# Turning the second attention's queries on VectorE and by way of memory, with scores one step later

## The reference, cut to what matters

```python
def _L1_xattn_ref(text, features, Wq_w, Wq_b, Wk_w, Wk_b, fn_w, qn_w, kn_w):
    features_n = rmsnorm(features, fn_w)
    Q = rmsnorm(jnp.einsum('btd,fd->btf', text, Wq_w) + Wq_b, qn_w)
    K = rmsnorm(jnp.einsum('bsd,fd->bsf', features_n, Wk_w) + Wk_b, kn_w)
    scores = jnp.einsum('btf,bsf->bts', Q, K) * (1.0 / jnp.sqrt(512))
    attn = softmax(scores)
    return jnp.einsum('bts,bsf->btf', attn, features_n)

x = x + tanh(g_xattn[1]) * _L1_xattn_ref(_layernorm(x), ctx, ...)
x = x + tanh(g_ffn[1]) * _L1_ffn_ref(_layernorm(x), ...)
```

## Time and profile before

| | us |
|---|---|
| median of 3 runs (956.25 to 958.32) | 958.04 |
| the profiled execution, its own time | 957.18 |
| its span on the core | 955.4 |
| query loop on TensorE, first matmul to the last `attended` in it | 861.6 to 900.9 |
| end of the last matmul | 952.1 |

### The profile page before, as it was taken

The page is one execution under the profiler, slowest core; times in us unless marked ns, Lnnn a source line. Parts: engine busy times, 40 slices in busy tenths (PEclk is TensorE's granted clock), DMA queues, the critical chain, the costliest instruction groups (busy, mean ns, idle before and its releaser), DMA issues.

```text
span 955.4 us, 15358 instructions
## 1 busy us (share of the span) xinstructions
PE 938.4 (98%) x4818; PEld 790.3 (83%) x4818; DVE 594.3 (62%) x1020; ACT 403.7 (42%) x1088; POOL 497.2 (52%) x463
## 2 busy tenths in 40 slices
PE   9999899999999999999999999999999999999998
PEld 7888688788878887888888888888888888888885
DVE  4788845385538553854476546664576967756754
ACT  5765424352434233433334334433442336657730
POOL 3857753454446453746374636563546335698630
PEclk9999999999999999999999999999999999999999
DMA  7146676875687667776777676866786565232002
GB/s 284 45 147 227 233 254 247 264 267 200 240 270 276 226 241 252 269 259 241 242 259 270 251 235 231 292 241 233 251 280 251 221 227 190 121 105 94 1 1 89
DMA packets 71412, 203.64 MB, mean 213 GB/s; under 512 B 10192, under 2 KB 24784, under 8 KB 70352
## 3 DMA queue, kind: packets, MB, share of 16 engines
q1 hardware_dynamic: 70368, 201.87, 59.3%
q10 hardware_dynamic: 1008, 1.32, 0.4%
HBM read 176.95 MB, written 26.21 MB: 213 GB/s over the span
## 4 chain that ended last, share of the span: by engine, by line
PE 72%; DMA 9%; DVE 9%; POOL 3%; issue 3%; ACT 2%; SPq 2%; DVEq 0%; POOLq 0%; ACTq 0%
PE bank L1965 22%; PE bank L2042 16%; PE bank L1981 9%; DMA keyed<-passing 7%; PE bank L2146 7%; PE bank L2014 6%; PE bank L1998 5%; PE bank L1941 3%; DVE turned_blocks L1435 2%; SPq L452 1%; DVE kt L1475 1%; PE bank L2170 1%; DVE turned_blocks L1439 1%; PE bank L2026 1%; PE bank L2291 1%
## 5 line engine op out<-in xcount | busy, mean ns | idle before, releaser
L2042 PE MATMUL bank<-wvo,ao 128*128 128x512 f32 x768 | 179.8, 391 | 0.6 <-issue 0.6
L1981 PE MATMUL bank<-wvo,ct 128*128 128x512 f32 x768 | 177.8, 390 | 0.0
L1981 PEld LDWEIGHTS bank<-wvo,ct 128*128 128x128 f32 x768 | 143.5, 188 | 29.4
L2042 PEld LDWEIGHTS bank<-wvo,ao 128*128 128x128 f32 x768 | 142.9, 188 | 29.8 <-issue 0.7
L629 POOL TENSOR_TENSOR wvo<-stage,wvo 128x512 fp32r<-128x512 f32 x64 | 85.0, 1350 | 149.6 <-ACT wvo L932 149.6
L1965 PE MATMUL bank<-ring,wkq 128*128 128x512 f32 x648 | 157.3, 390 | 0.0
L1965 PEld LDWEIGHTS bank<-ring,wkq 128*128 128x128 f32 x648 | 121.2, 188 | 25.1
L1453 DVE SCALAR_TENSOR_TENSOR acc<-bank,gated_rows,acc 128x512 f32<-128x512 f32 x128 | 93.2, 742 | 39.3 <-PE bank L2042 38.3
L978 ACT ACTIVATE bank<-bank,nmax 128x128 f32<-128x128 f32 x256 | 88.3, 351 | 55.6 <-DVE nmax L1415 55.6
L1444 DVE TENSOR_TENSOR ao<-bank,ao 128x512 fp32r<-128x512 f32 x64 | 43.9, 691 | 107.1 <-ACT ao L984 107.1
L1475 DVE TENSOR_TENSOR qt<-bank,qt 128x512 f32<-128x512 f32 x98 | 66.4, 690 | 57.1 <-PE bank L1965 55.7
(11 more groups left out here) (186 smaller groups left out, 1508.9 us busy)
## 6 DMA issues: line engine op xcount, KB each, us to landing
ring<-combined SPq DMA_DIRECT2D x216, 512.0 KB, 6.4
stage<-in_w SPq DMA_DIRECT2D x63, 512.0 KB, 4.2
passing<-turned_blocks SPq DMA_DIRECT2D x24, 512.0 KB, 2.9
keyed<-passing SPq DMA_DIRECT2D x96, 128.0 KB, 3.2
combined<-work SPq DMA_DIRECT2D x16, 512.0 KB, 3.6
xraw<-in_x SPq DMA_DIRECT2D x2, 1024.0 KB, 11.8
bias<-in_bias SPq DMA_DIRECT2D x8, 256.0 KB, 4.6
cs<-in_ctx SPq DMA_DIRECT2D x1, 2048.0 KB, 7.7
```

What stands on the lines that cost most here:

```text
L1981: mm = pe.matmul(bank[un_of[m][u] % RING][:, :], ct[:, i, c, b * P:(b + 1) * P], wvo[:, j, c, :], start=(c == 0 and i + j == 0), stop=(c = ...
L2042: mm = pe.matmul(bank[to][:, :], ao[:, h, p, b * P:(b + 1) * P], wvo[:, j, 2 * pair + h, :], start=(h == 0 and p + j == 0), stop=(h == 1 a ...
```

## The change

The four TensorE transposes and the ScalarE copy of each query tile are taken out. `query(u)` now writes `qbr` without regrouping (the regrouping is in the way the next step reads). VectorE turns the tile in 32 by 32 blocks into a new buffer `qtb` with two places (`query_turned(u)`). SyncE stores each tile to `passing_queries` (512 pieces of 512 B), waits until it has landed, and issues four reads of 32 partitions into `qtr`, now with four places. These instructions stand in SyncE's list behind the loop over the keys and ahead of the stores of the result. `query_turned(u)` waits, from u = 2 on, until the store of tile u - 2 has landed. In `qtr` the four chunks of features are interleaved, so that `scored` now loads its 128 by 128 operand with a step of 16 B between neighbours, where they were next to each other.

Everything from the scores on comes one step later: `scored` lags three steps, `probs_turned` four, `attended` five, and the steps of the other engines likewise. After the loop, one more step of each is done, and `base(0)` and `base(1)` come earlier in relation to the scores of tile 7 and the attention of tile 6.

```diff
+                sp.wait_ge(S["k_mm"], B)
+                for u in range(B):
+                    sp.wait_ge(S["q_T"], u + 1)
+                    sp.dma_start(passing_queries[u, :, :, :, :].rearrange("i k j c -> (i k) j c"),
+                                 qtb[:, u % 2, :, :, :].rearrange("p j t c -> p j (t c)")).then_inc(s_qpassed, 16)
+                    if u >= 4:
+                        sp.wait_ge(S["s_mm"], u - 3)
+                    sp.wait_ge(s_qpassed, B + 16 * u + 16)
+                    for j in range(4):
+                        sp.dma_start(qtr[32 * j:32 * j + 32, u % 4, :, :].rearrange("k (i t) c -> k i (t c)", i=4),
+                                     passing_queries[u, :, :, j, :].rearrange("i k c -> k i c")).then_inc(S["q_out"], 16)
...
-                def query_out(u):
-
-                    act.wait_ge(S["q_T"], u + 1)
-                    if u >= 2:
-                        act.wait_ge(S["s_mm"], u - 1)
-                    act.activation(qtr[:, u % 2, :, :], bank[6][:, :].rearrange("p (c t) -> p c t", c=KC),
-                                   ACT.Copy).then_inc(S["q_out"], 1)
...
+                    dve.tensor_tensor(qbr[:, u % 2, :], bank[2 + u % 2][:, :], rows[:, R_BQ, :], ALU.add).then_inc(S["q_b"], 1)
+
+                def query_turned(u):
+
+                    dve.wait_ge(S["q_b"], u + 1)
+                    if u >= 2:
+
+                        dve.wait_ge(s_qpassed, B + 16 * (u - 1))
+                    dve.transpose(qtb[:, u % 2, :, :, :].rearrange("p j t c -> p j c t"),
+                                  qbr[:, u % 2, :].rearrange("p (j c k) -> p j c k", j=4, c=KC)).then_inc(S["q_T"], 1)
...
-                def queries_turned(u):
-
-                    pe.wait_ge(S["q_b"], u + 1)
-                    if u:
-                        pe.wait_ge(S["q_out"], u)
-                    else:
-                        pe.wait_ge(s_dev, x1_done(6))
-                    turned(6, qbr[:, u % 2, :], "q_T")
-
                 def scored(u):
 
-                    pe.wait_ge(S["q_out"], u + 1)
+                    pe.wait_ge(S["q_out"], 64 * u + 64)
...
-                        mm = pe.matmul(bank[0][:, 0:P], qtr[:, u % 2, c, :], kt1[:, u // 2, :, c, u % 2 * 32:u % 2 * 32 + 32],
+                        mm = pe.matmul(bank[0][:, 0:P], qtr[:, u % 4, :, c], kt1[:, u // 2, :, c, u % 2 * 32:u % 2 * 32 + 32],
```

More of the change, by code:

```diff
@@ L183, in build @@
     passing_keys = nc.dram_tensor("passing_keys", (B // 2, 4, 32, 4, KC * 2 * 32), fp32, kind="Internal").ap()
+    passing_queries = nc.dram_tensor("passing_queries", (B, 4, 32, 4, 32 * KC), fp32, kind="Internal").ap()
     expanded = nc.dram_tensor("expanded", (P, KC, D), fp32, kind="Internal").ap()
@@ L217, in build @@
     wra = nc.alloc_sbuf_tensor_at("wra", [P, 2, KC, RAW], fp32r, offset=xr_at)
+    qtr = nc.alloc_sbuf_tensor_at("qtr", [P, 4, P, KC], fp32, offset=xr_at + 8192)
     wt_f = place("wt_f", [P, 2, KC, D], fp32r)
@@ L232, in build @@
     qbr = place("qbr", [P, 2, D], fp32)
-    qtr = place("qtr", [P, 2, KC, P], fp32)
+    qtb = place("qtb", [P, 2, 4, 32, KC], fp32)
     wexp = place("wexp", [P, HB, NEXP, ROUT], fp32)
@@ L327, in build @@
         s_kpassed, s_kback = s_mneg, s_k0
+        s_qpassed = s_css
         half = lambda s: slice(s * 512, s * 512 + 512)
@@ L876, in _ @@
                         split_lo("ra", u - 1)
-                for u in range(4, B):
+                for u in range(3, B):
                     add_row(u - 1, R_BASE, "xn2", "rsb")
@@ L1321, in _ @@
                 probs_out(6)
+                normed(4, 2)
                 normed(5, 2)
@@ L1601, in query @@
                         dve.wait_ge(S["q_ss"], u - 1)
-                    dve.tensor_tensor(qbr[:, u % 2, :].rearrange("p (c j k) -> p j c k", c=KC, j=4),
-                                      bank[2 + u % 2][:, :].rearrange("p (j c k) -> p j c k", j=4, c=KC),
-                                      rows[:, R_BQ, :].rearrange("p (j c k) -> p j c k", j=4, c=KC), ALU.add).then_inc(S["q_b"], 1)
+                    dve.tensor_tensor(qbr[:, u % 2, :], bank[2 + u % 2][:, :], rows[:, R_BQ, :], ALU.add).then_inc(S["q_b"], 1)
[5 more added lines that the diff above has]
+                                  qbr[:, u % 2, :].rearrange("p (j c k) -> p j c k", j=4, c=KC)).then_inc(S["q_T"], 1)
                 def scores_max(u):
@@ L1821, in _ @@
                     query(u)
+                    query_turned(u)
                     if u < 6:
@@ L1827, in _ @@
                         key_turned(7)
-                    if u >= 2:
-                        scores_max(u - 2)
-                    if u >= 4:
-                        x3(u - 4)
-                    if u >= 2:
-                        scores_sum(u - 2)
-                    if u >= 4:
-                        stats1(u - 4, 2)
+                    if u >= 3:
+                        scores_max(u - 3)
+                    if u >= 5:
+                        x3(u - 5)
+                    if u >= 3:
+                        scores_sum(u - 3)
+                    if u >= 5:
+                        stats1(u - 5, 2)
+                scores_max(5)
+                x3(3)
+                scores_sum(5)
+                stats1(3, 2)
                 lo(1, 2)
@@ L2256, in adapters @@
                     elif u == 2:
-                        pe.wait_ge(S["q_out"], B)
+                        pe.wait_ge(s_dev, x1_done(6))
                     elif u == 3:
@@ L2311, in _ @@
                         T(0, 2)
-                    if u:
-                        queries_turned(u - 1)
-                    if u >= 2:
-                        scored(u - 2)
                     if u >= 3:
-                        probs_turned(u - 3)
+                        scored(u - 3)
                     if u >= 4:
-                        attended(u - 4)
+                        probs_turned(u - 4)
+                    if u >= 5:
+                        attended(u - 5)
+                scored(5)
+                probs_turned(4)
+                attended(3)
                 T(1, 2)
                 adapters(0)
-                queries_turned(7)
                 scored(6)
@@ L2327, in _ @@
                 adapters(1)
+                base(0)
                 scored(7)
@@ L2330, in _ @@
                 attended(5)
-                base(0)
                 T(3, 2)
+                base(1)
                 probs_turned(7)
@@ L2335, in _ @@
                 attended(6)
-                base(1)
                 adapters(3)
```

25 lines of the change are left out of this document (12 added, 13 removed).

## The result

The changed kernel takes 970.9 us (median of 4 runs, 969.9 to 973.6) where the kernel before took 958.1 on the same chip: a ratio of 1.0137, 95% interval 1.0112 to 1.0161, 12.8 us slower. The profiled execution took 969.9 us, its span is 968.1. The forecast was 964.3 with a range of 960 to 970: the sign held, but the loss is twice the 6.3 us forecast, and the time is 0.9 us outside the range.

A forecast was written before the change was run, and what follows sets the result against it. TensorE's list was taken as the bound, paced by SyncE's query transfers: new waits of nearly 10 us less 3.5 for transposes end it 6.3 later, 958.0 + 6.3 = 964.3 us, range 960.0 to 970.0.

The forecast's parts named there:

- What bounds the kernel: TensorE, busy 98% of the span: in the query loop a matmul removed is time won, a new wait time lost.
- SyncE's transfers pace TensorE at tiles 5 and 6: End of the query loop: serial query transfers make TensorE wait again; tile 6 decides, last matmul at 958.4 us.
- The sum after `scored(0)`: TensorE's work from the start of the first scores to the end of the last matmul: 72.5 us.
- The transposes, -3.5: TensorE's path in the query loop: four transposes removed per tile save 0.44 us, eight tiles 3.5 us.
- The weight load: Rival, scores on TensorE: loads with the 16 B step make a pair take 0.22 us, 968 in all; chance 0.18.
- VectorE's strided row: Profile row cited against slow strided access: a VectorE operation writing every eighth word, 64 of them, takes 0.22 us.
- The rival's second sum: Scores on TensorE, load and matmul without any overlap: 0.30 us a pair, giving 968 and 15 us.
- The first wait, 5.9: Before the first scores: TensorE is ready at 876.6 us, the first query there at 882.5, a wait of 5.9 us.
- The rate of the queries, 4.5: SyncE's queue: each query takes 2.3 us to store and 2.2 to issue its reads, a period of 4.5 us.
- The store's 2.6 us: A query's store to memory by the Trainium skill's rule, 2.6 us, beside the 2.3 that the forecast took.
- The clock: TensorE's clock was at the full level in all 40 slices, so the forecast counted no term for it.
- Its wait for the stores: VectorE's turning of a query waits for the store of tile u - 2; claimed to cost nothing while reads are slow.

The follow-up runs named there:

- quarter kernel: The kernel before with one of the four TensorE transposes of each query tile, three left out: 953.9 us, ratio 0.9969.
- the join is soon: The kernel after with chunks kept apart, ScalarE's joining copy ahead of its exponentials, the weighting of the last keys later: 966.0 us.
- the best kernel: The kernel after with chunks apart, joined by ScalarE ahead of exponentials, first queries' transfers ahead of the last keys, some VectorE work later: 957.1 us.

## Why the prediction was right in its sign and short in its size

**What bounds the kernel: right.** TensorE's list sets the end, and each wait or longer operation on it is lost one for one. Its other half, that SyncE's transfers pace TensorE at tiles 5 and 6, did not come true (below). The sum after `scored(0)` shows how well: I counted 72.5 us to the end. With 7.8 for the scores, 1.1 for the clock and 0.3 for the exponential that is 81.7, and the trace has 964.67 - 882.09 = 82.6 (the last two matmuls end 0.87 after 963.80). In the kernel with the first query earlier, 72.5 + 7.8 + 0.3 = 80.6 stands against 81.4. Both miss by the same 0.8 to 0.9. About half is VectorE's second late `lo`, behind `scored(0)` and not in this sum, 0.45 us at 929.4 in the kernel after. The rest fits the order of the list, of which the forecast said "only in another order, so I use it as it is". Over the whole loop, from the start of one group to the next, the sixteen records of `attended` take 1.5 us more than before, the products 1.1 less (the clock's share taken out), the other groups 0.4 more: 0.9 in all. With it the 14.5 us close: scores 7.7, waits 8.3, clock 1.1, order 0.9, transposes -3.4 (rounded).

**The transposes, -3.5: right.** The quarter kernel bears it out, within its spread.

**The weight load: the step that failed.** The forecast put the step of 16 B among the rivals with a chance of 0.18, "Against it: VectorE's strided row". The price that the rival named was close (a pair at 0.22, 7.1 us in all; it took 0.233, 7.8 us), and its total was 968. The forecast itself left the scores at 0.89 us a tile, that is, it put the term at nothing, for no better reason than VectorE's row, and so ended at 964.3 where 970.9 was measured. That row is an operation of 64 elements that writes with a step; no row had the same operation without one, and none had a load with a step. Measured alone, in the kernel before, the step costs 7.7 us. The sign that the prediction named for it, pairs of 0.2 us or more, is what the trace shows. (The rival's second sum, without any overlap, comes to 967.2 and not 968; the 15 us beside it are right.) The Trainium skill's rule (SBUF — State Buffer, Door 1: The DMA port swizzle) that reads want two hits in each line of 16 B agrees with the trace (192 to 327 ns); the same page's statement that a step of four fp32 is free doesn't.

**The first wait, 5.9: right in size (6.6), by other terms.** Taken from the start of the loop, TensorE was ready for `scored(0)` 0.7 us later than forecast, and the query was there 1.3 later. The store of the first query took 4.9 us instead of 2.3 (5.0 in the second execution). It stands right behind four reads of keys, 512 KB in all, and data moved at 225 to 254 GB/s until some 2.6 us after the store's issue:

```profile
873.50:875.50 2.00, 2.00 (x11) 1.00 0.97 254
875.50:876.50 1.00, 0.02 (x1) 1.00 0.67 225
876.50:877.50 1.00, 0.00 (x0) 1.00 0.01 2
```

(The kernel after; window, its length, PE busy, PEclk, DMA share, GB/s.) Then next to nothing moves until the store has landed, 2.3 us later. The later stores, which stand behind four reads of 64 KB, landed in 2.0 to 2.2. But the place behind the keys' reads doesn't give 4.9 each time. In four other kernels with the same order in SyncE's list the reads took 2.8 to 3.1 us to issue and the store 2.75 to 2.84 to land; here the one with the chunks kept apart:

```profile
876.58 2.77 SPq L614 DMA_DIRECT2D kt<-passing_keys  x4
879.45 0.38 SPq L620 DMA_DIRECT2D passing_queries<-qtb  x1
882.20 1.73 SPq L626 DMA_DIRECT2D qtr<-passing_queries  x4
```

From the first read of keys to the store's landing it is 5.6 to 6.0 us in these four and 6.8 in both executions of the kernel after. The place costs at least some 0.6 us; what the quiet 2.3 us are stays open. The forecast took the long issue (2.74) with a short landing (2.3), 5.0 in all. Against that the last read landed in 1.96, not 2.65, and SyncE reached the first store 0.6 earlier than forecast, counted from the loop's start, since its reads of keys went out in 1.73. That my 5.9 held is luck: these errors ran against each other.

**The rate of the queries, 4.5: wrong.** The stores are 4.0 apart (2.2 to the reads, 1.77 to issue them). The store's 2.6 us that the prediction sets beside its own from the Trainium skill (DMA: Bandwidth & Descriptors, Anatomy of one DMA) would have made it longer still, and the trace disagrees, with 2.0 to 2.2 for the later stores. I had taken 2.74 us of issuing into a mean, which occurs once in a while, and 2.3 for the store. Tiles 5 and 6 therefore don't decide, tile 0 does, and the 3.4 us that the forecast had for them (958.4 against 955.0) were not there. This error made the forecast look better than its parts.

**The clock: a term left out.** "So no term here comes from the clock" was read from a trace in which TensorE never waited long. The change that I forecast had a wait of 6 us in it, and 1.1 us follows from that.

**VectorE.** Its wait for the stores is harmless, as said: TensorE waits for the same store. The block transposes are not 0.68 but 1.12 us each with the step of 16 B, which the forecast had put at nothing by the same row. So `lo(2, 1)` is later than the 0.6 us forecast, TensorE's order in time:

```profile
868.92 2.97 PE L2169 MATMUL bank<-wt_q,tt 128*128 128x512 f32 x12 [1.05 <-DVE tt L1579]
```

**What went unforeseen beside TensorE.** Between two scores stand VectorE's maximum and ScalarE's exponential. Where TensorE's work between them gets shorter, TensorE waits for that chain: 0.3 us in the kernel after, 0.9 and 1.0 before `scored(5)` in the two kernels where the scores are short and the join is soon. In the best kernel VectorE shares in it: the scores of tile 4 end at 896.2, and the maximum starts at 896.80, behind a `lo`. The chain, `lo` and the new order of the list together give back what the transposes brought, and so the repaired kernel ends level with the one before and not below it. That the transposes had been the cover for the chain is not shown: with three quarters of them gone and the lag unchanged no such wait appeared, which speaks for the place of `scored(5)` in the new order. Whether the wait can be filled is open too, since both kernels that tried it made another wait by their own moves.

## What to carry to other kernels

Before you change the layout of an operand that TensorE loads, measure such a load by itself: here a step of 16 B made each load 1.7 times as long and cost more than twice what the transposes had. A row of another engine, or of a much smaller operation, is no evidence for it. Work taken from the engine that sets the end is worth its time only as long as no wait comes up in its place, and the same matmuls in another order need not take the same time. A transfer that is the first of its kind in a serial queue should be priced with what stands in flight ahead of it, and a wait of several microseconds on TensorE with the clock behind it.

## What the runs showed of the chip that I had not expected

- A weight load of 128 by 128 fp32 takes 192 ns unstrided and 327 ns with 16 B from one element to the next; a pair of load and matmul goes from 0.11 to 0.23 us, and with the step it is 0.23 at the lower clock too.
- The same step on writes: VectorE's block transpose of 128x512 takes 1.12 us instead of 0.71, ScalarE's copy out of a bank 1.09 instead of 0.59.
- TensorE's clock was at its lower level behind waits of 6.3 to 6.7 us and behind one of 2.25 us (in two kernels), and stayed at the full level behind waits of 0.3 to 1.95 us.
- A store of 256 KB mostly landed in 2.0 to 2.4 us. Right behind the four reads of 128 KB it took 2.75 to 2.84 us in four kernels and 4.9 and 5.0 in the two executions of the kernel after; the last store of the loop, with only reads of 64 KB ahead of it, took 4.2 and 4.4 in two others.
- Four reads take SyncE 1.73 us to issue in most cases, but now and then 2.5 to 3.3.
